# Last layer: the weighted sum of the gathered rows moved from GpSimd to VectorE, supertiles 1 to 7

## The chip, the cores and the metric

The kernel runs on one core of a Trainium2 chip, as one launch. The metric is the device time of that launch in microseconds (us). Three timed runs of the kernel before gave 674.5 us as the median, with 672.77 and 675.93 as the lowest and highest. The core has a matrix engine (TensorE, PE in the profile), VectorE (DVE), ScalarE (ACT), GpSimd (POOL) and SyncE (SP), which issues most DMAs. Each engine works through its own list of instructions in order; between engines, and between dependent instructions of one engine, the kernel waits on counting semaphores.

## The reference

A decoder block on 4096 tokens of width 128, float32: attention, a mixture of experts with two of eight experts for each token (routed by a second input, ctx), and a second mixture with eight of 32 experts and a shared expert. Each is applied to the normalised x and added to x.

```
x = x + attention(layernorm(x))
x = x + sum over the token's 2 experts of  weight * expert(layernorm(x))      # the sum that is moved
x = x + (sum over 32 experts of  c[t, e] * down_e(silu(gate_e(h)) * up_e(h)) + shared(h)),   h = layernorm(x)
```

The second line's last step is what the change touches: for each token t, `x[t] += w0[t] * y0[t] + w1[t] * y1[t]`, where y0 and y1 are the rows that its two experts computed. These lie in DRAM, sorted by expert (`y_sorted`), and are gathered by indirect DMA.

## The kernel before

**Tiling.** Tokens lie on the 128 partitions; 32 tiles of 128 tokens make up 8 supertiles of 512 (four tiles, TPS). `x_all` (128 x 32 x 128) holds x for the whole run. The last layer is a double loop over supertiles i = 0 to 7 and, within each, p = 0 to 16: 16 pairs of experts and the shared one (NC2 = 17). In a step n = 17 i + p TensorE makes a gate and an up product of three passes each (L1638 to L1640, over 128x512), ScalarE takes the silu of the gate (`r_s`, L975), VectorE multiplies it with the up product (`gated`, L1433: `rc_s`) and with the token weights (`weighted`, L1446: `t_s`; the shared expert has a plain copy instead, L1441). TensorE multiplies the result with the down weights; where it is split in a high and a low part (p from 5 to 16 in supertiles 1 to 6), ScalarE writes `t_h` (L740) and VectorE `t_l` (L1505) in front of that. TensorE may make the up product of step n only when `gated` of step n - 3 has freed its bank.

**Preparation of the next supertile.** While supertile i runs, the inputs of supertile j = i + 1 are prepared at steps fixed by the tables `SLOTS` and `FIRST` (L94, L98), each engine doing its part in its list at that step. For j of 2 and more:

- i = j - 2, early: GpSimd gathers the rows of j (`gather`, L682, 8 indirect DMAs, L688) into `yg[:, j % 2]`, then adds them to `x_all` (`combine(j, h)`, L700, for the two halves h of a supertile: 4 multiplications of 128x128, L705, and 2 additions of 128x256, L707, each with a wait for the one in front of it).
- i = j - 2, p = 14: VectorE waits for the sum and takes statistics of the four tiles (`row_statistics(j, 0)` and `(j, 1)`, L1346, BATCH_NORM_STATS2); at p = 15 `aggregate(j)` (L1352, BATCH_NORM_AGGREGATE) and GpSimd's `rstd(j)` (L693, an addition and a power).
- i = j - 1, p = 0: VectorE writes `nb`, the negated mean times the root (L1364). p = 1: ScalarE normalises four tiles (`xnp`, L918). p = 2: the expert weights of supertile j - 1 are turned and copied by ScalarE (`cT`, L740). p = 3: TensorE waits for `xnp` and for `cT` and turns `xnp` (L1540), ScalarE copies the result to `fxh` and VectorE makes its low part `fxl`. p = 6 to 12: the routing of j, with the routing's small instructions on VectorE at p = 9 to 12.

For j = 1 the same steps stand at p = 4 and later of supertile 0 (`FIRST`), and `combine(1, h)` is in front of them in GpSimd's list. Supertile 0 itself was combined in the layer before by VectorE (`combine_first`, L1448, 8 SCALAR_TENSOR_TENSOR at L1454, each computing weight times row plus x, with a wait behind each). GpSimd's list in the last layer holds `gather`, `combine` and `rstd` in the order gather(i + 2), combine(i + 2), rstd(i + 2). A `gather(j)` waits until the sum of j - 2 has freed its buffer.

Of the kernel before, what the change touches and what calls it, by code (L numbers as in the profile page):

```python
# [21 lines left out]
ALU = mybir.AluOpType  # L22
# [8 lines left out]
NS = T // ST  # L31
TPS = ST // P
# [69 lines left out]
def steps_at(i, p):  # L102

    steps = [(name, 1) for name, s in FIRST.items() if divmod(s, NC2) == (i, p)]
    return steps + [(name, j) for name, s in SLOTS.items() if name not in ("accS", "tp", "x2")
                    for j in [i + 1 - s // NC2] if s % NC2 == p and 2 <= j < NS]
# [52 lines left out]
def decoder_kernel(nc, x, ctx_in, W_DQ, b_DQ, W_UQ, b_UQ, W_DKV, b_DKV, W_UK, b_UK, W_UV, b_UV, W_QR, b_QR,  # L159
# [17 lines left out]
    with ExitStack() as stack:  # L177
# [11 lines left out]
        x_all = sb("x_all", [P, NT, D])  # L189
# [12 lines left out]
        wts = sb("wts", [P, NT, 2])  # L202
# [81 lines left out]
        yg = a("yg", [P, 2, TPS, 2, D])  # L284
# [44 lines left out]
        def sem(name):  # L329
            return stack.enter_context(nc.semaphore(name))  # L330
# [12 lines left out]
        s_yg = [[sem(f"gathered{i}_{h}") for h in range(2)] for i in range(2)]  # L343
# [19 lines left out]
        F = {n: sem("f2_" + n) for n in (  # L363
            "up gate act rc t th tl dn accS tp x2 cmb1 cmb bst pstat prstd pnb pxn pxT_ps fxh xT fxl lg lgS back sc cw c_ps cT "
            "chain").split()}
# [174 lines left out]
        def _(pool):  # L540
            ch = Chain(pool, s_pchain)
# [140 lines left out]
            def gather(j, t):  # L682
                if t == 0 and j <= 2:
                    stored(min(E1 * (j + 1), NBK))
                if j >= 2 and t == 0:
                    pool.wait_ge(F["cmb"], TPS + 2 * (j - 2))
                for c in range(2):
                    pool.indirect_dma_start(  # L688
                        out=yg[:, j % 2, t, c, :], out_offset=None, in_=ys,
                        in_offset=bass.IndirectOffsetOnAxis(ap=posi[:, j * TPS + t, c:c + 1], axis=0))\  # L690
                        .then_inc(s_yg0[t] if j == 0 else s_yg[j % 2][t // 2], 16)

            def rstd(j):  # L693

                pool.wait_ge(F["pstat"], j + 1)
                pool.tensor_tensor(mvp[:, :, 1], mvp[:, :, 1], meps[:, :], ALU.add).then_inc(F["prstd"], 1)  # L696
                pool.wait_ge(F["prstd"], 2 * j + 1)
                pool.tensor_tensor(mvp[:, :, 1], mvp[:, :, 1], mhalf[:, 0:TPS], ALU.pow).then_inc(F["prstd"], 1)

            def combine(j, h):  # L700
                pool.wait_ge(s_yg[j % 2][h], 64 * ((j + 1) // 2))
                t = slice(j * TPS + 2 * h, j * TPS + 2 * h + 2)
                for c in range(2):
                    for u in (2 * h, 2 * h + 1):
                        ch.done(pool.tensor_scalar(yg[:, j % 2, u, c, :], yg[:, j % 2, u, c, :],  # L705
                                                   wts[:, j * TPS + u, c:c + 1], 0.0, ALU.mult, ALU.add))
                    ins = pool.tensor_tensor(x_all[:, t, :], x_all[:, t, :], yg[:, j % 2, 2 * h:2 * h + 2, c, :], ALU.add)  # L707
                    if c == 0:
                        ch.done(ins)
                ins.then_inc(F["cmb"], 1)  # L710

            for b in range(2, NBK):
                w_high(b, 0)
                w1_low(b)
# [5 lines left out]
                    rstd(0)  # L720
            for t in range(TPS):
                gather(1, t)
            for h in range(2):
                combine(1, h)
            rstd(1)
            for i in range(NS):
                for p in range(NC2):
                    for name, j in steps_at(i, p):
                        if name == "prstd":
                            rstd(j)  # L730
                    if i + 2 < NS and p % 2 == 0 and p < 8:
                        gather(i + 2, p // 2)
                    if i + 2 < NS and p in (8, 9):
                        combine(i + 2, p - 8)


        @block.scalar
        def _(act):
# [49 lines left out]
            def normalise1(m, t):  # L788

                if m >= 2 and t == 0:  # L790
                    act.wait_ge(A["xT"], m - 1)
                at = m * TPS + t
                for part, (first, _) in enumerate(PARTS):
                    if at == first:
                        act.wait_ge(s_rstd1, part + 1)
                ins = act.activation(xn[:, m % 2, t, :], x_all[:, at, :], ACT.Identity, bias=nm1[:, at:at + 1],
                                     scale=mv1[:, at, 1:2])
                if t == TPS - 1:
                    ins.then_inc(A["xn"], 1)
# [214 lines left out]
        def _(dve):  # L1014
            tt, ts = dve.tensor_tensor, dve.tensor_scalar
            ch = Chain(dve, s_dchain)
# [269 lines left out]
            for n in range(-LEAD, NT + TAIL):  # L1286
# [3 lines left out]
                o, u, m = n - LAG["out"], n - LAG["sum"], n - LAG["xs"]  # L1290
# [53 lines left out]
            pc = Chain(dve, F["chain"])  # L1344

            def row_statistics(j, h):  # L1346
                dve.wait_ge(F["cmb"], TPS + 2 * (j - 1) + h + 1)
                for t in (2 * h, 2 * h + 1):
                    ins = dve.bn_stats(st6p[:, t, :], x_all[:, j * TPS + t, :])
                ins.then_inc(F["bst"], 1)  # L1350
# [62 lines left out]
            def route_weights(j):  # L1413
# [5 lines left out]
                if j >= 1:  # L1419
# [3 lines left out]
                    .then_inc(F["cw"], 1)  # L1423

            prep = dict(cmbA=lambda j: row_statistics(j, 0), cmbB=lambda j: row_statistics(j, 1), paggr=aggregate, pnb=negated_mean,
                        fxl=low_x, rt_a=route_groups, rt_b=route_rank, rt_c=route_experts, rt_d=route_weights)

# [58 lines left out]
            for n in range(NCB + LAG1 + 1):  # L1486
                b, c = n // FB, n % FB
# [507 lines left out]
```

## Time and profile before

| | before |
|---|---|
| median of three timed runs | 674.5 us |
| profiled execution, its own time | 673.04 us |
| its span (first to last instruction) | 671.0 us |
| TensorE busy | 618.0 us (92% of the span) |
| VectorE busy | 538.6 us (80%) |
| ScalarE busy | 422.2 us (63%) |
| GpSimd busy | 344.7 us (51%) |
| mean granted TensorE clock | 0.972 of full speed |

The last layer fills the span from about 354 us to its end. A page of the profile gives busy time by engine, the span in 40 slices, the DMA queues, the chain of work that ended last and the costliest groups of instructions. Instructions of one engine are pipelined: a new one can start before the record of the one in front ends, so the time that an instruction costs its engine is read from start to start. A row of the timeline gives the start in us, the duration in us, the engine and line, the operation, what it writes and reads, and in square brackets how long the engine was idle in front of it and what ended that.

### The profile page before, as it was taken

The numbers are of one execution on the slowest core, as the hardware profiler recorded it, in microseconds if no ns is written. First come the engines' busy times: TensorE is split into PE (matmuls) and PEld (weight loads), VectorE is DVE, ScalarE is ACT, GpSimd is POOL, SyncE is SP. The second block draws the span as 40 slices with busy tenths as digits, with TensorE's granted clock in tenths as the row PEclk, the third lists the DMA queues.
The fourth block names the chain that finished last, engine by engine and source line by source line (L and its number), as shares of the span: only waits on it lengthen the run. The fifth ranks groups of instructions, "written<-read, shape, count | busy, mean of one in ns | idle before, by whom it ended". The sixth has DMA issues, their size and how long they took to land.

```text
span 671.0 us, 11543 instructions
## 1 busy us (share of the span) xinstructions
PE 618.0 (92%) x3354; PEld 462.8 (69%) x3354; DVE 538.6 (80%) x1357; ACT 422.2 (63%) x779; POOL 344.7 (51%) x410
## 2 busy tenths in 40 slices
PE   8878888887879999999889999999999999999997
PEld 8655565554658888787667656776777767677873
DVE  4787799998866666876665778899999999989973
ACT  3674668764469998898875444665737465473530
POOL 6134868888775657864567672643808265000000
PEclk9988779999779999999999999999999999999999
DMA  8997013102445555554217543534536354434561
GB/s 224 311 384 246 17 60 96 33 32 64 107 111 156 163 174 167 179 165 149 81 60 195 127 99 113 152 101 133 138 108 164 96 155 117 133 106 127 146 157 32
DMA packets 77836, 90.20 MB, mean 134 GB/s; under 512 B 15361, under 2 KB 44011, under 8 KB 77774
## 3 DMA queue, kind: packets, MB, share of 16 engines
q1 hardware_dynamic: 72648, 80.96, 42.2%
q0 software_dynamic: 4288, 8.40, 4.4%
q8 instruction: 27, 0.44, 0.3%
q14 instruction: 35, 0.29, 0.1%
q10 hardware_dynamic: 838, 0.11, 0.1%
HBM read 64.48 MB, written 24.90 MB: 133 GB/s over the span
## 4 chain that ended last, share of the span: by engine, by line
PE 62%; POOL 11%; DVE 7%; issue 5%; ACT 2%; DMA 1%; DVEq 0%; ACTq 0%; POOLq 0%
PE bank L1638 10%; PE bank L1640 9%; PE bank L1639 9%; PE pair_banks L1929 7%; PE pair_banks L1540 5%; POOL x_sorted L613 5%; PE score_banks L1638 4%; PE score_banks L1640 4%; PE score_banks L1639 4%; PE pair_banks L1638 2%; PE pair_banks L1640 2%; PE pair_banks L1639 2%; POOL yg L688 2%; POOL sm L597 1%; DMA yg<-y_sorted,posi 1%
## 5 line engine op out<-in xcount | busy, mean ns | idle before, releaser
L975 ACT ACTIVATE r_s<-bank 128x512 f32<-128x512 f32 x136 | 80.7, 595 | 68.2 <-PE bank L1640 66.4
L1446 DVE TENSOR_TENSOR t_s<-rc_s,bcb 128x512 f32<-128x512 f32 x128 | 89.0, 698 | 4.8 <-PE pair_banks L1929 4.8
L613 POOL DMA_INDIRECT x_sorted<-xsb,posi x64 | 64.0, 1000 | 27.8 <-issue 14.8
L688 POOL DMA_INDIRECT yg<-y_sorted,posi x64 | 68.4, 1068 | 18.1 <-issue 17.7
L1433 DVE TENSOR_TENSOR rc_s<-r_s,score_banks 128x512 f32<-128x512 f32 x90 | 61.2, 680 | 17.9 <-ACT r_s L975 14.6
L1638 PE MATMUL bank<-fxh,Gh 128*128 128x512 f32 x136 | 73.2, 538 | 0.0
L740 ACT ACTIVATE t_h<-t_s 128x512 fp32r<-128x512 f32 x72 | 45.3, 629 | 41.3 <-DVE t_s L1446 26.6
L1929 PE MATMUL pair_banks<-t_s,Dn 128*128 128x512 f32 x128 | 63.2, 591 | 0.0
L1505 DVE TENSOR_TENSOR t_l<-t_s,t_h 128x512 fp32r<-128x512 f32 x72 | 54.9, 763 | 0.2
L1640 PE MATMUL bank<-fxh,Gl 128*128 128x512 f32 x136 | 53.7, 395 | 0.0
L1639 PE MATMUL bank<-fxl,Gh 128*128 128x512 f32 x136 | 53.4, 392 | 0.0
L1495 DVE TENSOR_TENSOR h1l<-bank,h1h 128x512 fp32r<-128x512 f32 x46 | 31.8, 691 | 21.9 <-ACT bank L962 21.9
L1495 DVE TENSOR_TENSOR h1l<-score_banks,h1h 128x512 fp32r<-128x512 f32 x46 | 31.8, 690 | 20.2 <-ACT score_banks L962 20.1
L696 POOL TENSOR_TENSOR mvp<-mvp,meps 128x4 f32<-128x4 f32 x8 | 1.6, 204 | 86.8 <-DVE mvp L1356 86.8
L597 POOL TENSOR_TENSOR sm<-sm,rden 128x512 f32<-128x512 f32 x29 | 30.2, 1043 | 19.1 <-DVE rden L1302 18.9
L740 ACT ACTIVATE uS<-pair_banks 128x256 f32<-128x256 f32 x32 | 12.3, 383 | 41.2 <-PE pair_banks L1725 36.1
L664 POOL TENSOR_SCALAR W2h<-wraw 128x512 fp32r<-128x512 f32 x21 | 13.0, 618 | 47.7 <-PE bank L1640 47.6
L1433 DVE TENSOR_TENSOR rc_s<-r_s,bank 128x512 f32<-128x512 f32 x46 | 31.3, 680 | 6.8 <-ACT r_s L975 5.6
L961 ACT ACTIVATE h1h<-score_banks,bcur 128x512 fp32r<-128x512 f32 x46 | 31.9, 694 | 7.0 <-PE score_banks L1640 3.3
L1638 PE MATMUL score_banks<-fxh,Uh 128*128 128x512 f32 x90 | 35.7, 396 | 0.6 <-DVE rc_s L1433 0.6
L1638 PEld LDWEIGHTS bank<-fxh,Gh 128*128 128x128 f32 x136 | 25.6, 188 | 15.4 <-issue 11.6
L1638 PE MATMUL bank<-h1h,W2h 128*128 128x512 f32 x92 | 36.1, 393 | 0.0
(335 smaller groups left out, 1847.3 us busy)
## 6 DMA issues: line engine op xcount, KB each, us to landing
bcb<-c_rows SPq DMA_DIRECT2D x128, 256.0 KB, 4.0
wraw<-in_L_xattn_W SPq DMA_DIRECT2D x46, 256.0 KB, 3.0
x_sorted<-wraw SPq DMA_DIRECT2D x1, 5888.0 KB, 18.3
y_sorted<-wraw SPq DMA_DIRECT2D x1, 5888.0 KB, 33.8
xg<-x_sorted SPq DMA_DIRECT2D x23, 256.0 KB, 2.6
y_sorted<-ysb SPq DMA_DIRECT2D x23, 256.0 KB, 2.0
ctxb<-in_ctx SPq DMA_DIRECT2D x8, 256.0 KB, 5.8
out<-x_all SPq DMA_DIRECT2D x8, 256.0 KB
```

The lines of the kernel that those rows point to most:

```text
L613: pool.indirect_dma_start(out=xs, out_offset=bass.IndirectOffsetOnAxis(ap=posi[:, m, c:c + 1], axis=0), in_=xsb[:, m % SC, :], in_offset=N ...
L688: pool.indirect_dma_start(out=yg[:, j % 2, t, c, :], out_offset=None, in_=ys, in_offset=bass.IndirectOffsetOnAxis(ap=posi[:, j * TPS + t, ...
L740: return act.activation(dst, src, ACT.Copy)
L975: act.activation(r_s[:, n % RB2, :], bank[n % 3][:, :], ACT.Silu).then_inc(F["act"], 1)
L1433: tt(rc_s[:, n % CB2, :], r_s[:, n % RB2, :], bank[3 + n % 3][:, :], ALU.mult).then_inc(F["rc"], 1)
L1446: tt(t_s[:, n % TB2, :], rc_s[:, n % CB2, :], bcb[:, p - 1, :], ALU.mult).then_inc(F["t"], 1)
L1495: tt(h1l[:, n % NB1, :], gate_bank1(n)[:, :], h1h[:, n % NB1, :].bitcast(F32), ALU.subtract)\
L1505: tt(t_l[:, k % HB2, :], t_s[:, m % TB2, :], t_h[:, k % HB2, :].bitcast(F32), ALU.subtract)\
L1638: mm(dst, wh, xh, start=start, stop=False)
L1639: mm(dst, wh, xl, start=False, stop=False)
L1640: return mm(dst, wl, xh, start=False, stop=stop)
L1929: ins = mm(bank[6][:, :], Dn[:, weights_of(p), :], t_s[:, n % TB2, :], start=(p == 0), stop=(p == NC2 - 1))
```

## The change

For supertiles 1 to 7 `combine` is taken out of GpSimd's list, definition and calls. `row_statistics(j, h)` on VectorE first waits for the gathered half, then issues four SCALAR_TENSOR_TENSOR of 128x128 (weight times row plus x, in place in `x_all`): two for the first expert, a wait, two for the second, and a wait in front of its two BATCH_NORM_STATS2. With two halves that makes eight such instructions and four waits for a supertile. They stand at p = 14 of supertile j - 2, and at p = 4 of supertile 0 for j = 1. `gather` and `rstd` stay on GpSimd, in the same order; all semaphores keep their counts.

```diff
--- before.py
+++ after.py
@@ -697,18 +697,6 @@
-            def combine(j, h):
-                pool.wait_ge(s_yg[j % 2][h], 64 * ((j + 1) // 2))
-                t = slice(j * TPS + 2 * h, j * TPS + 2 * h + 2)
-                for c in range(2):
-                    for u in (2 * h, 2 * h + 1):
-                        ch.done(pool.tensor_scalar(yg[:, j % 2, u, c, :], yg[:, j % 2, u, c, :],
-                                                   wts[:, j * TPS + u, c:c + 1], 0.0, ALU.mult, ALU.add))
-                    ins = pool.tensor_tensor(x_all[:, t, :], x_all[:, t, :], yg[:, j % 2, 2 * h:2 * h + 2, c, :], ALU.add)
-                    if c == 0:
-                        ch.done(ins)
-                ins.then_inc(F["cmb"], 1)
-
@@ -720,8 +708,6 @@
             for t in range(TPS):
                 gather(1, t)
-            for h in range(2):
-                combine(1, h)
             rstd(1)
@@ -730,8 +716,6 @@
                     if i + 2 < NS and p % 2 == 0 and p < 8:
                         gather(i + 2, p // 2)
-                    if i + 2 < NS and p in (8, 9):
-                        combine(i + 2, p - 8)
@@ -1344,6 +1328,15 @@
             def row_statistics(j, h):
+                dve.wait_ge(s_yg[j % 2][h], 64 * ((j + 1) // 2))
+                for c in range(2):
+                    for t in (2 * h, 2 * h + 1):
+                        xr = x_all[:, j * TPS + t, :]
+                        ins = dve.scalar_tensor_tensor(xr, yg[:, j % 2, t, c, :], wts[:, j * TPS + t, c:c + 1], xr,
+                                                       ALU.mult, ALU.add)
+                    if c == 0:
+                        pc.done(ins)
+                ins.then_inc(F["cmb"], 1)
                 dve.wait_ge(F["cmb"], TPS + 2 * (j - 1) + h + 1)
```

## Rows read from the trace of the kernel before

**Rows 1.** The page, busy us (share of span) xinstructions, TensorE and VectorE.

```profile
PE   618.0 (92%) x3354; PEld 462.8 (69%) x3354; DVE 538.6 (80%) x1357; ACT 422.2 (63%) x779; POOL 344.7 (51%) x410
```

**Rows 2.** Busy time by stretch: start:end, length, then us (xinstructions) of each engine.

```profile
core 0: us, PE busy (x) PEld busy (x) DVE busy (x) ACT busy (x) POOL busy (x), PEclk, DMA share, GB/s
493.00:532.00 39.00, 37.97 (x167) 28.76 (x166) 37.14 (x99) 22.74 (x41) 19.36 (x22) 1.00 0.49 130
...
571.00:610.00 39.00, 37.98 (x168) 28.66 (x167) 35.54 (x100) 22.66 (x42) 1.23 (x2) 1.00 0.45 119
```

**Rows 3.** Chain that ended last: start us, us, what; the turns at p = 3 and 14.

```profile
508.43 0.63 PE pair_banks L1540 x4
...
532.83 0.44 PE pair_banks L1540 x4
...
586.60 0.63 PE pair_banks L1540 x4
...
611.00 0.44 PE pair_banks L1540 x4
```

**Rows 4.** Timeline of all engines, supertile 3 p = 14 to supertile 4 p = 3.

```profile
498.84 0.87 DVE L1349 BATCH_NORM_STATS2 st6p<-x_all 128x6 f32<-128x128 f32 x4
...
505.28 0.17 DVE L1364 SCALAR_TENSOR_TENSOR nb<-mvp 128x4 f32<-128x4 f32 x1
...
505.48 1.65 ACT L918 ACTIVATE xnp<-x_all,nb,mvp 128x128 f32<-128x128 f32 x4 [1.37 <-DVE nb L1364]
...
508.03 0.26 ACT L740 ACTIVATE cT<-pair_banks 128x128 f32<-128x128 f32 x1
...
508.16 0.69 DVE L1433 TENSOR_TENSOR rc_s<-r_s,bank 128x512 f32<-128x512 f32 x1 [0.92 <-ACT r_s L975]
...
508.43 0.63 PE L1540 MATMUL pair_banks<-ident,xnp 128*128 128x128 f32 x4 [1.03 <-ACT cT L740]
```

**Rows 5.** Timeline of VectorE: the shared expert's copy in three supertiles, and an idle stretch.

```profile
406.94 0.77 DVE L1441 COPY t_s<-rc_s 128x512 f32<-128x512 f32 x1
...
446.25 0.42 DVE L1441 COPY t_s<-rc_s 128x512 f32<-128x512 f32 x1
...
523.43 0.69 DVE L1433 TENSOR_TENSOR rc_s<-r_s,score_banks 128x512 f32<-128x512 f32 x1 [0.38 <-ACT r_s L975]
524.04 0.83 DVE L1441 COPY t_s<-rc_s 128x512 f32<-128x512 f32 x1
```

**Rows 6.** Timeline of VectorE: SCALAR_TENSOR_TENSOR in the layer before, and in the routing.

```profile
267.82 0.96 DVE L1454 SCALAR_TENSOR_TENSOR x_all<-yg,wts,x_all 128x128 f32<-128x128 f32 x2
268.81 0.29 DVE L1457 BATCH_NORM_STATS2 st6p<-x_all 128x6 f32<-128x128 f32 x1
...
287.63 0.73 DVE L1454 SCALAR_TENSOR_TENSOR x_all<-yg,wts,x_all 128x128 f32<-128x128 f32 x2
288.39 0.29 DVE L1457 BATCH_NORM_STATS2 st6p<-x_all 128x6 f32<-128x128 f32 x1
...
497.44 0.29 DVE L1421 SCALAR_TENSOR_TENSOR cw<-rep,csum 128x128 f32<-128x128 f32 x1
497.64 0.68 DVE L1433 TENSOR_TENSOR rc_s<-r_s,score_banks 128x512 f32<-128x512 f32 x1
```

**Rows 7.** Timeline in supertile 0: VectorE's waits for the sums, GpSimd's for data.

```profile
360.67 0.48 DVE L1349 BATCH_NORM_STATS2 st6p<-x_all 128x6 f32<-128x128 f32 x2 [1.04 <-POOL x_all L707]
...
379.87 0.84 POOL L705 TENSOR_SCALAR yg<-yg,wts 128x128 f32<-128x128 f32 x2 [0.34 <-DMA yg<-y_sorted,posi]
...
383.63 0.49 DVE L1349 BATCH_NORM_STATS2 st6p<-x_all 128x6 f32<-128x128 f32 x2 [0.69 <-POOL x_all L707]
```

**Rows 8.** Timeline at the start of supertile 2: ScalarE's copy and the turn.

```profile
428.75 0.28 ACT L740 ACTIVATE cT<-pair_banks 128x128 f32<-128x128 f32 x1
...
430.64 0.60 PE L1540 MATMUL pair_banks<-ident,xnp 128*128 128x128 f32 x4
```

**Rows 9.** Timeline at the start of supertiles 1, 3, 5 and 6: the same turn.

```profile
392.10 0.63 PE L1540 MATMUL pair_banks<-ident,xnp 128*128 128x128 f32 x4 [0.98 <-ACT cT L740]
...
469.31 0.63 PE L1540 MATMUL pair_banks<-ident,xnp 128*128 128x128 f32 x4 [0.60 <-ACT cT L740]
...
547.51 0.63 PE L1540 MATMUL pair_banks<-ident,xnp 128*128 128x128 f32 x4 [1.01 <-ACT cT L740]
...
586.60 0.63 PE L1540 MATMUL pair_banks<-ident,xnp 128*128 128x128 f32 x4 [1.02 <-ACT cT L740]
```

## The prediction

> **What bounds the kernel now.** I read the page's busy times first, then the busy time by stretch, then the chain that ended last, then the timeline around each idle place of TensorE. TensorE is busy for 92% of the span [rows 1], and in the last layer for 37.97 us of 39 [rows 2]; VectorE shows 37.14 of 39 in the same stretch. So both are nearly full, and the question is where they are coupled. The chain gives the answer: it runs over TensorE except at one place in each supertile, the turn of `xnp` at p = 3. In rows 3 the turn at p = 3 is followed by the turn at p = 14 after 24.40 us (508.43 to 532.83, and 586.60 to 611.00), and that one by the next p = 3 after 14.69 us (532.83 to 547.51 in rows 9); together 39.09 us for a supertile.
>
> Rows 4 show what happens in the 14.69 us. VectorE takes the statistics at 498.84, writes `nb` at 505.28; ScalarE, idle for 1.37 us, starts `xnp` 0.20 us later; behind it in its list stand `t_h`, a silu and `cT`, which ends at 508.29; TensorE, idle for 1.03 us, turns `xnp` 0.14 us after that. Each step waits for the one in front. And VectorE is not idle between its catching up at 523.43 (the counterpart one supertile later, [rows 5]) and `nb`: the routing at p = 9 to 12 makes it late, and its next idle time is only the 0.92 us behind `nb` [rows 4]. So whatever is put into VectorE's list at p = 14 delays `nb`, the turn and with it TensorE, one for one. That idle time of TensorE is 0.98, 0.60, 1.03, 1.01 and 1.02 us at the start of supertiles 1, 3, 4, 5 and 6 [rows 4, 9], and none at the start of supertile 2, where `cT` ended at 429.03 and the turn came at 430.64 [rows 8]. With the 0.14 us of the others, that one has 1.47 us to spare.
>
> **The added work.** Eight SCALAR_TENSOR_TENSOR of 128x128 for each supertile. The same instruction with the same operands is in the trace, in the layer before: two of them, each with a wait behind it, take 0.76 us from start to start (287.63 to 288.39) while GpSimd idles, so 0.38 each [rows 6]. A wait costs some 0.12 of that: the routing's SCALAR_TENSOR_TENSOR of 128x128, 0.29 long, is followed after 0.20 by an instruction that needn't wait for it [rows 6]; taking that overlap of 0.09 and the 0.03 between end and next start off 0.38 leaves 0.26 without a wait (an estimate from these rows). Eight instructions, four with a wait: 4 x 0.38 + 4 x 0.26 = 2.56 us. The low end takes the routing's instruction, which has no pointer to a weight, 0.20 without and 0.29 + 0.03 with a wait: 2.1 us. The high end takes the pair that ran beside GpSimd's own work, 0.99 us for two (267.82 to 268.81), with every one waiting: 4.0 us. I take 2.56, since at p = 14 GpSimd only waits for VectorE. The statistics themselves stay, in two pairs in place of one four.
>
> **The removed work.** GpSimd loses 4 multiplications and 2 additions for each half. It has no wait behind it on the path, except in supertile 0: there VectorE waited 1.04 us (j = 1) and 0.69 us (j = 2) for the sum [rows 7]. Both waits go. Nothing else becomes late instead: GpSimd found the last half of j = 2 landed at 379.87, and VectorE wants it 2.6 us later and more. `gather(j)` for later j is issued behind `rstd(j - 1)`, so ahead of the `nb` at 505.28, for data wanted one supertile after the 498.84 of rows 4, over 30 us later. The waits that VectorE now makes on gathered data are therefore already met; behind one stand `gated` and all of TensorE, if I am wrong.
>
> **What GpSimd no longer disturbs.** While its multiplications and additions run, VectorE's instructions on two SBUF tensors, and its copy, take longer: the shared expert's copy takes 0.83 us at 524.04 and 0.77 at 406.94, against 0.42 at 446.25 [rows 5]. In sum VectorE is busy 37.14 us in a supertile with GpSimd's sums and 35.54 in one without, for as many instructions [rows 2]: 1.6 us. Only what lies behind VectorE's catching up counts for `nb`, and that is the copy: 0.41 us in supertiles 3 to 5, 0.35 in supertile 1, nothing in 2. The rest lies ahead of an idle stretch of VectorE, and the distance of 24.40 us from p = 3 to p = 14 is the same with the sums (508.43 to 532.83) and without (586.60 to 611.00) [rows 3].
>
> The Trainium skill (SBUF — State Buffer, section "SBUF: two separate sides") says that VectorE with two SBUF inputs and GpSimd lock each other out for a whole instruction. The trace agrees (the copy at 0.83 against 0.42). By that rule alone all 1.6 us of each supertile would come back; by rows 3 they do not reach TensorE. The rule's own result is the second rival.
>
> **The sum**, for the delay of TensorE:
> - j = 1, supertile 0, p = 4: 2.56 - 1.04 = 1.5 us. `nb` and the turn follow each other tightly there too.
> - j = 2, supertile 0, p = 14: 2.56 - 0.69 = 1.85 us (disturbances in supertile 0 not counted).
> - j = 3, supertile 1: 2.56 - 0.35 - 1.47 of spare time = 0.75 us.
> - j = 4, supertile 2: 2.56 us.
> - j = 5, 6, 7, supertiles 3 to 5: 3 x (2.56 - 0.41) = 6.45 us.
>
> Together 13.1 us. The delays don't overlap: each supertile's comes after VectorE has caught up, which it does between, since the 24.40 us from p = 3 to p = 14 hold idle time of VectorE and 1.2 us more of it than before. TensorE may show part of the new idle time earlier, as a wait for `gated` at p = 0 or 1 (its bank is freed three steps later), but not on top of it. Against the profiled execution's own 673.04 us that is 686.1; against the median of 674.5, 687.6. I take 686.5 us, 1.8% above the median.
>
> **The rivals.**
> - *The price is the low one* (2.1 us): 7 x 0.48 = 3.4 us less, 683 us. For it: 0.20 from start to start at this size [rows 6]. Against: the same instruction with its pointer had 0.38.
> - *The relief counts in full.* The 1.6 us of each of supertiles 1 to 5 come off, not 0.41: supertile 1 costs nothing, supertiles 2 to 5 0.96 each, with 3.35 of supertile 0: 7.2 us, 680.2 us. Needed for it: that VectorE's idle stretch at 523.43 is made by VectorE itself (ScalarE's `t_h` waits for `t_s`), so that all moves up. Against: the equal 24.40 us of rows 3.
> - *The price is the high one*, or a further wait comes on top, as for gathered data: 4.0 us each, 1.4 x 7 = 10 us more, 696 us.
> - *Faster*: GpSimd's late sums are what counted, and the additions on VectorE are hidden. Then 1.04 + 0.69 of waits [rows 7] and 0.35 + 3 x 0.41 of the copy go, 3.3 us, 669.7 us. It decides from the point at which VectorE has 2.56 us of idle time between the statistics and `nb`; the trace shows none there, and 0.92 us behind `nb`.
> - *No change*: idle time of VectorE behind `nb` and ahead of the routing takes most of the work, and what is left equals the 3.3 us: 674 us. It needs TensorE's idle time at the turn to have another cause than `nb`, as `cT`; but `cT` stands behind `xnp` in ScalarE's list, and ScalarE waited 1.37 us for `nb` [rows 4].
>
> **How the numbers follow.** Forecast (684 to 690 us) 0.62, low price 0.14, full relief 0.08, high price 0.07, no change 0.05, faster 0.04. The range from 680 to 691 us holds the first three, 0.84. About 0.5% is what a measurement of this kernel can tell from no change. Over 0.5% faster (below 671.1): 0.04. Within: 0.06, no change and a bit of the others. Slower: 0.90.
>
> **What would show it.** In the changed kernel: eight SCALAR_TENSOR_TENSOR at p = 14 that cost VectorE about 2.6 us; VectorE never idle from there to `nb`; ScalarE idle ahead of `xnp`; TensorE idle for about 3.2 us in front of or shortly ahead of the turn in supertiles 3 to 6, and 41.2 us from turn to turn there in place of 38.7 (430.64 to 469.31) and 39.1; the copy at 0.42 us everywhere; no wait of VectorE on a gather. The prediction is wrong if the turns stay 39.1 us apart (something hides the work), if the statistics come late because a gather does, or if the instructions take 0.2 or 0.5 us.

## The result and the profile after

The changed kernel takes 686.3 us (median of six timed runs, 684.56 to 687.62) against 673.69 us for the kernel before in the same measurement: a ratio of 1.0181, with a 95% interval of 1.0156 to 1.0206, so 12.6 us slower. The forecast was 686.5.

| | before | after |
|---|---|---|
| profiled execution's span | 671.0 us | 685.9 us |
| TensorE busy | 618.0 | 625.2 |
| VectorE busy | 538.6 | 546.3 |
| GpSimd busy | 344.7 | 288.0 |

The first lines of the page of the changed kernel (busy us, share of span, count; rows 1 before):

```profile
span 685.9 us, 11515 instructions
...
PE 625.2 (91%) x3354; PEld 465.7 (68%) x3354; DVE 546.3 (80%) x1413; ACT 422.2 (62%) x779; POOL 288.0 (42%) x326
```

VectorE has the 56 instructions more, and only 7.7 us more of busy time. The two spans differ by 14.9 us, 2.3 more than the medians. 1.45 us of that lie ahead of the layer that was changed (its first `gated` starts at 355.44 after 353.99), where the changed kernel has the same instructions. The granted TensorE clock differed there between the two executions (0.93 of full speed from 100 to 200 us before, and 0.88 after); that this makes the 1.45 us is likely, but not shown. From the first `gated` to the end it is 317.0 us before and 330.5 after: 13.4 us more.

The next rows are the turns of `xnp` at p = 3 in the changed kernel, on TensorE, at the start of supertiles 1 to 4 and 6 (rows 4, 8 and 9 before; the number in brackets is the idle time ahead):

```profile
396.56 0.63 PE L1533 MATMUL pair_banks<-ident,xnp 128*128 128x128 f32 x4 [0.96 <-ACT cT L724]
...
436.03 0.63 PE L1533 MATMUL pair_banks<-ident,xnp 128*128 128x128 f32 x4 [0.74 <-ACT cT L724]
...
477.31 0.63 PE L1533 MATMUL pair_banks<-ident,xnp 128*128 128x128 f32 x4 [1.62 <-ACT cT L724]
...
518.56 0.63 PE L1533 MATMUL pair_banks<-ident,xnp 128*128 128x128 f32 x4 [1.61 <-ACT cT L724]
...
601.48 0.63 PE L1533 MATMUL pair_banks<-ident,xnp 128*128 128x128 f32 x4 [1.60 <-ACT cT L724]
```

From 436.03 to 477.31 and from there to 518.56 it is 41.28 and 41.25 us, where the kernel before took 38.67 and 39.12. The timeline between, all engines, from p = 13 of supertile 3 to p = 3 of supertile 4 (the counterpart of rows 4):

```profile
505.78 0.68 DVE L1439 TENSOR_TENSOR t_s<-rc_s,bcb 128x512 f32<-128x512 f32 x1
...
506.38 1.26 DVE L1335 SCALAR_TENSOR_TENSOR x_all<-yg,wts,x_all 128x128 f32<-128x128 f32 x4
...
507.68 0.49 DVE L1342 BATCH_NORM_STATS2 st6p<-x_all 128x6 f32<-128x128 f32 x2
...
508.08 1.25 DVE L1335 SCALAR_TENSOR_TENSOR x_all<-yg,wts,x_all 128x128 f32<-128x128 f32 x4
...
509.36 0.49 DVE L1342 BATCH_NORM_STATS2 st6p<-x_all 128x6 f32<-128x128 f32 x2
...
510.49 0.50 PE L1631 MATMUL score_banks<-fxh,Uh 128*128 128x512 f32 x1 [0.94 <-DVE rc_s L1426]
...
515.42 0.16 DVE L1357 SCALAR_TENSOR_TENSOR nb<-mvp 128x4 f32<-128x4 f32 x1
...
515.61 1.65 ACT L902 ACTIVATE xnp<-x_all,nb,mvp 128x128 f32<-128x128 f32 x4 [1.36 <-DVE nb L1357]
...
518.16 0.26 ACT L724 ACTIVATE cT<-pair_banks 128x128 f32<-128x128 f32 x1
```

Four additions take 1.30 and 1.28 us from start to start, 2.58 for a supertile, and none waits for gathered rows. `nb` follows the first addition after 9.04 us; before, it followed the first statistics after 6.44 [rows 4]: 2.60 us more. ScalarE waits for `nb` as before (1.36 us), `cT` ends 0.14 us ahead of the turn as before. TensorE shows its new idle time in two places, 0.94 us for the `gated` that follows the additions and 0.58 more at the turn. These are 1.5 of the 2.1 us by which this supertile is longer (41.25 against 39.12); the other 0.6 us lie mostly in TensorE's own records, which show it busy for 38.6 us from turn to turn in place of 38.1 (the row at 510.49 shows 0.50 us, its counterpart before 0.39).

VectorE's counterpart of rows 5, one supertile on:

```profile
533.60 0.69 DVE L1426 TENSOR_TENSOR rc_s<-r_s,score_banks 128x512 f32<-128x512 f32 x1 [1.91 <-ACT r_s L959]
534.20 0.42 DVE L1434 COPY t_s<-rc_s 128x512 f32<-128x512 f32 x1
```

The copy is back at 0.42 us, and the idle time ahead of the `gated` in front of it has grown from 0.38 to 1.91 us: VectorE spends in idling what it no longer loses to GpSimd there, and then works without a pause into the turn.

### The profile page after: what moved, and what is told of

Read it like the earlier page. It is cut to its first block, busy times and chain, and to the rows that moved or that the text cites. A ratio compares the mean times of both kernels' runs of the same rounds, so it can differ in the third digit from the quotient of the medians.

```text
span 685.9 us, 11515 instructions
## 1 busy us (share of the span) xinstructions
PE 625.2 (91%) x3354; PEld 465.7 (68%) x3354; DVE 546.3 (80%) x1413; ACT 422.2 (62%) x779; POOL 288.0 (42%) x326
## 4 chain that ended last, share of the span: by engine, by line
PE 53%; DVE 19%; issue 7%; POOL 6%; ACT 3%; DMA 0%; DVEq 0%; ACTq 0%; POOLq 0%
PE bank L1631 8%; PE bank L1633 8%; PE bank L1632 8%; PE pair_banks L1922 5%; PE pair_banks L1533 5%; POOL x_sorted L613 4%; PE score_banks L1631 4%; PE score_banks L1633 3%; PE score_banks L1632 3%; DVE t_s L1439 2%; DVE x_all L1335 2%; DVE rc_s L1426 2%; PE pair_banks L1631 2%; PE pair_banks L1633 2%; PE pair_banks L1632 2%
## 5 line engine op out<-in xcount | busy, mean ns | idle before, releaser
L1439 DVE TENSOR_TENSOR t_s<-rc_s,bcb 128x512 f32<-128x512 f32 x128 | 87.3, 684 | 4.8 <-PE pair_banks L1922 4.8
L1498 DVE TENSOR_TENSOR t_l<-t_s,t_h 128x512 fp32r<-128x512 f32 x72 | 49.2, 684 | 0.2
L1633 PE MATMUL bank<-h1h,W2l 128*128 128x512 f32 x92 | 36.0, 392 | 0.0
```

Source lines behind the costliest of these rows:

```text
L1439: tt(t_s[:, n % TB2, :], rc_s[:, n % CB2, :], bcb[:, p - 1, :], ALU.mult).then_inc(F["t"], 1)
L1498: tt(t_l[:, k % HB2, :], t_s[:, m % TB2, :], t_h[:, k % HB2, :].bitcast(F32), ALU.subtract)\
L1633: return mm(dst, wl, xh, start=False, stop=stop)
```

## The experiments

Ten kernels, in three groups (half, double, nosum and ghost; pool12, the two nb_early kernels and sum_p8; the last two), each beside the kernel before on the same chip. The chips differ: the kernel before takes 673.75 us on that of the second group and 687.5 and 687.2 us on those of the first and the third. So each time is read against its own kernel before, as a ratio, and the expectations, which are given for a kernel before of 673.7 us, are turned into ratios. The changed kernel itself ran only on its first chip, so a comparison of another kernel with it goes over two ratios. A ratio comes from the single runs with its interval, and differs from the quotient of the two medians by up to 0.0016. The distance from turn to turn, from supertile 2 on, gives no sign of the difference between the chips; this table is worked out from the timelines of TensorE (us; "2 to 3": from the turn at the start of supertile 2 to that of 3).

| kernel | 2 to 3 | 3 to 4 | 4 to 5 | 5 to 6 | ratio to before (95%) |
|---|---|---|---|---|---|
| before | 38.67 | 39.12 | 39.08 | 39.09 | 1 |
| after | 41.28 | 41.25 | 41.46 | 41.46 | 1.0181 (1.0156 to 1.0206) |
| half | 39.97 | 39.98 | 39.97 | 39.98 | 1.0061 (1.0032 to 1.0090) |
| double | 43.90 | 43.89 | 43.90 | 44.41 | 1.0475 (1.0432 to 1.0519) |
| nosum | 38.98 | 38.99 | 39.00 | 39.01 | 1.0005 (0.9977 to 1.0033) |
| ghost | 42.06 | 41.77 | 42.51 | 42.25 | 1.0273 (1.0229 to 1.0316) |
| pool12 | 41.35 | 41.27 | 41.26 | 41.27 | 1.0152 (1.0107 to 1.0197) |
| nb_early_after | 39.78 | 39.80 | 39.95 | 40.00 | 1.0075 (1.0049 to 1.0101) |
| nb_early_before | 37.91 | 38.46 | 38.14 | 38.12 | 0.9940 (0.9915 to 0.9964) |
| sum_p8 | 39.17 | 39.31 | 39.29 | 39.31 | 1.0054 (1.0031 to 1.0078) |
| sum_p8_nb | 38.06 | 38.23 | 38.20 | 38.23 | 0.9977 (0.9946 to 1.0009) |
| pool12_p8_nb | 38.08 | 38.18 | 38.22 | 38.25 | 0.9937 (0.9906 to 0.9968) |

**Is it the additions?** Half of them, and twice as many. half leaves the second expert's rows out of the sum, double adds every row twice; neither computes the reference. The comments in the code shown from here on are added for the reader.

```
-                for c in range(2):
+                for c in range(1):                                   # half (its wait goes too)
+                for r, c in ((0, 0), (0, 1), (1, 0), (1, 1)):        # double (a wait behind each pair but the last)
```

> The changed kernel with the second expert's four additions of each supertile left out of the sum (so four instead of eight SCALAR_TENSOR_TENSOR, no wait between them). Theory (VectorE's list from its catching up to nb passes into TensorE's time one for one): 1.28 us less in each of six supertiles and the 0.93 us of supertile 1, 8.6 us less than the changed kernel's 686.3: about 677.7 us. Rival (VectorE loses its time waiting for gathered rows, not with the additions): no change, 686 us.

> The changed kernel with the whole sum made twice (16 additions for a supertile, a wait behind each group of two; x gets the rows twice). Theory: 2.56 us more in each of seven supertiles, 18 us more than 686.3: about 704 us. Rival (the 12.6 us of the change are a single cost for having moved the sum, such as the waits for gathered data): under 2 us more.

Measured: 1.0061 and 1.0475; expected were 677.7 / 673.7 = 1.0059 and 704 / 673.7 = 1.045. Half takes 1.3 us off the distance of the turns from supertile 2 to 4 (41.27 to 39.97), and double adds 2.6 (43.90). From 4 to 6, where the changed kernel has 41.46, it is 1.5 less and 2.4 to 3.0 more. On VectorE two additions with one wait take 0.64 us from start to start in half, and eight with four waits 2.60 in double: again 1.3 us for four. half still waits for the gathered rows, and yet the cost fell, and it rose with the number of additions. So neither a wait for these rows nor a one-time cost makes it.

**What did GpSimd's work cost?** Taken from both engines (nosum, which leaves the sum out and so doesn't compute the reference), and given back to GpSimd with nobody reading it (ghost).

```
# nosum, in row_statistics, in place of the four additions of a half
+                dve.memset(spare[:, :], 0.0).then_inc(F["cmb"], 1)
# ghost, on GpSimd for j = 2 to 7, where combine was
+                        ch.done(pool.tensor_scalar(gh_a[:, u % 2, :], yg[:, j % 2, u, c, :],
+                                                   wts[:, j * TPS + u, c:c + 1], 0.0, ALU.mult, ALU.add))
+                    ch.done(pool.tensor_tensor(gh_a[:, :, :], gh_a[:, :, :], yg[:, j % 2, 2 * h:2 * h + 2, c, :], ALU.add))
```

> The changed kernel with the sum left out on both engines for supertiles 1 to 7 (VectorE still waits for the gathered rows and signals with a one-element memset). Theory: the eight additions less at 0.1 us for the two memsets: 6 x 2.45 + 0.93 = 15.6 us less than 686.3, about 670.7 us, that is 3 us under the kernel before (its two waits for GpSimd and the disturbed copies). Rival (GpSimd's work on SBUF slowed the whole supertile by the 1.6 us by which VectorE's busy time falls): 1.7 + 5 x 1.6 = 9.7 us under the kernel before, 664 us.

> The changed kernel with GpSimd also making the multiplications and additions of supertiles 2 to 7 as before, but into a buffer that nobody reads. Theory: only the disturbed copy of the shared expert counts, 0.35 + 3 x 0.41 = 1.6 us more than 686.3: 687.9 us; the turns at p = 3 stand 0.4 us further apart in supertiles 3 to 5. Rival (relief counts in full): 5 x 1.6 = 8 us more, 694 us.

Measured for nosum: 1.0005 (0.9977 to 1.0033), where 0.9955 was expected and 0.986 by the rival. So both were too low, the rival by far more. The turns tell why: 38.98 us against 39.09. The two memsets cost more than the 0.1 us I gave them. In VectorE's timeline of nosum (p = 13 and 14 of a late supertile):

```profile
513.60 0.69 DVE L1432 TENSOR_TENSOR t_s<-rc_s,bcb 128x512 f32<-128x512 f32 x1
514.24 0.06 DVE L1332 MEMSET spare<- 128x1 f32 x1
514.34 0.49 DVE L1335 BATCH_NORM_STATS2 st6p<-x_all 128x6 f32<-128x128 f32 x2
514.78 0.06 DVE L1332 MEMSET spare<- 128x1 f32 x1
514.89 0.49 DVE L1335 BATCH_NORM_STATS2 st6p<-x_all 128x6 f32<-128x128 f32 x2
515.29 0.67 DVE L1419 TENSOR_TENSOR rc_s<-r_s,score_banks 128x512 f32<-128x512 f32 x1
```

From `t_s` to the next `gated` it is 1.69 us, where the kernel before needs 0.60 and 0.78:

```profile
498.24 0.68 DVE L1446 TENSOR_TENSOR t_s<-rc_s,bcb 128x512 f32<-128x512 f32 x1
498.84 0.87 DVE L1349 BATCH_NORM_STATS2 st6p<-x_all 128x6 f32<-128x128 f32 x4
499.62 0.67 DVE L1433 TENSOR_TENSOR rc_s<-r_s,score_banks 128x512 f32<-128x512 f32 x1
```

That leaves 0.31 us for two memsets with their waits. The turns give the same number: from supertile 2 to 3, where the copy of the kernel before was not disturbed, nosum has 38.98 us against 38.67. In the later ones 39.09 - 0.41 + 0.31 is 38.99, as measured. So in a supertile whose copy was disturbed, GpSimd's sum had cost TensorE 0.4 us, not 1.6. The memsets explain 0.2 us more in each supertile than I had allowed, 1.3 of the 3.4 us that the ratio misses; the other 2 us are as much as the interval leaves open, and no row places them. They may lie in supertile 0, whose expected gain can't be read here: from the turn within supertile 0 (that of j = 1) to the next it is 31 to 34 us on this chip in all kernels of the group, and 27 to 29 on that of the second.

Measured for ghost: 1.0273 (1.0229 to 1.0316), where 1.021 was expected and 1.030 by the rival. So the time of the whole kernel fits the rival's number and not that of my theory. The turns fit neither: from the turn of supertile 1 to that of 6 it took 208.7 us against 204.9 in the changed kernel, 3.8 more, where my theory had 1.6 and the rival 8. By the ratios ghost is some 6 us slower than the changed kernel, with an uncertainty of several us; what is beyond the 3.8 isn't placed.

Supertile by supertile the 3.8 us are 0.62, 0.78, 0.52, 1.05 and 0.79. The copy explains only the third, as foreseen (0.92 us at 504.61, next start 0.84 behind it); in the other four it took 0.41 or 0.42 us. VectorE's timeline of ghost in the fourth:

```profile
537.89 0.69 DVE L1437 TENSOR_TENSOR rc_s<-r_s,bank 128x512 f32<-128x512 f32 x1 [1.26 <-ACT r_s L970]
...
540.90 1.23 DVE L1509 TENSOR_TENSOR t_l<-t_s,t_h 128x512 fp32r<-128x512 f32 x1
...
543.30 1.23 DVE L1509 TENSOR_TENSOR t_l<-t_s,t_h 128x512 fp32r<-128x512 f32 x1
544.46 0.68 DVE L1437 TENSOR_TENSOR rc_s<-r_s,bank 128x512 f32<-128x512 f32 x1
545.05 0.73 DVE L1450 TENSOR_TENSOR t_s<-rc_s,bcb 128x512 f32<-128x512 f32 x1
545.70 1.24 DVE L1509 TENSOR_TENSOR t_l<-t_s,t_h 128x512 fp32r<-128x512 f32 x1
546.86 0.68 DVE L1437 TENSOR_TENSOR rc_s<-r_s,score_banks 128x512 f32<-128x512 f32 x1
547.46 0.41 DVE L1445 COPY t_s<-rc_s 128x512 f32<-128x512 f32 x1
```

and TensorE's:

```profile
565.19 0.50 PE L1642 MATMUL score_banks<-fxh,Uh 128*128 128x512 f32 x1 [2.06 <-DVE rc_s L1437]
...
573.27 0.63 PE L1544 MATMUL pair_banks<-ident,xnp 128*128 128x128 f32 x4 [1.61 <-ACT cT L735]
```

There is no idle time ahead of the `gated` at 546.86, where the changed kernel has 1.91 us. VectorE's last idle time is now the 1.26 us at 537.89, and three disturbed `t_l` (1.23 and 1.24 us) lie behind it, which my theory had in front of it. TensorE idles for 2.06 us behind them, where the changed kernel has 1.10. So the place of the last idle time was the wrong premise here: it moves when the engine gets more work. How much of the disturbance behind it arrives stays open: three times 0.55 us would be 1.65, and the distance grew by 1.05. The Trainium skill (SBUF — State Buffer, section "SBUF: two separate sides") has a VectorE instruction with two SBUF inputs and a GpSimd instruction that reads SBUF lock each other out. The trace agrees with it in the single instruction (1.24 against 0.68 us for `t_l`), and whether that reaches the end of the kernel depends on the idle time. The copy, on which the prediction rested its agreement, reads one tensor; that it is disturbed as well is what the rows show.

**The terms of supertile 0.** Sums of supertiles 1 and 2 back on GpSimd (pool12):

```
+            for h in range(2):
+                combine(1, h)
...
+                    if i == 0 and p in (8, 9):
+                        combine(i + 2, p - 8)
...
+                if j >= 3:                                           # VectorE's additions
```

> The changed kernel with the sums of supertiles 1 and 2 back on GpSimd, where they were before; 3 to 7 on VectorE. Theory: the two terms of supertile 0 go, 1.48 + 1.53 = 3.0 us: 683.3 us. Rival (the cost arises in the later supertiles only, since supertile 0 holds idle time): 686.3 us.

Measured: 683.12 us against 673.75 there, 1.0152 (1.0107 to 1.0197); 683.3 was expected, a ratio of 1.0143, and 1.0187 by the rival. Both lie in the interval, so the time doesn't decide. The turns do. The first two are at 10.91 and 38.06 us from the layer's start, as before (10.92 and 38.11), and 12.40 and 41.12 in the changed kernel. The two terms together are 3.0 us, and the rival falls.

**Is `nb` to the turn the path, or is VectorE simply full?** One number, `pnb`, moves `nb` from p = 0 to p = 16 of the supertile in front, in both kernels:

```
-SLOTS = dict(cmbA=-3, cmbB=-3, paggr=-2, prstd=-2, pnb=0, ...)
+SLOTS = dict(cmbA=-3, cmbB=-3, paggr=-2, prstd=-2, pnb=-1, ...)
```

> The changed kernel with one number changed: nb goes from p = 0 to p = 16 of the supertile before in VectorE's list (pnb = -1), in front of the gated, weighted and t_l of that step. Theory (nb, xnp, cT and the turn are the path): nb 1.8 us earlier, xnp 1.36 us earlier, since ScalarE's silu ahead of it then ends last; that takes 1.36 us off the turn's idle time of 1.6 in supertiles 3 to 6, and the 0.74 and 0.96 of two others: 7.1 us less, about 679 us. Rival (VectorE's whole work in a supertile is the bound, wherever it stands): 686.3 us.

> The kernel before with the same one number changed (pnb = -1). Theory: TensorE's idle time at the turns goes, 0.98 + 0.60 + 1.03 + 1.01 + 1.02 = 4.6 us: 669.1 us against 673.7. Rival (another thing than nb holds the turn, as cT or the down products): no change.

Measured: 678.6 us and 669.73 us, against 679 and 669.1 expected and no change by the rivals. The timeline of nb_early_after, all engines:

```profile
507.02 1.03 POOL L698 TENSOR_TENSOR mvp<-mvp,mhalf 128x4 f32<-128x4 f32 x1
...
508.35 0.17 DVE L1357 SCALAR_TENSOR_TENSOR nb<-mvp 128x4 f32<-128x4 f32 x1
...
508.88 1.64 ACT L902 ACTIVATE xnp<-x_all,nb,mvp 128x128 f32<-128x128 f32 x4
...
511.42 0.26 ACT L724 ACTIVATE cT<-pair_banks 128x128 f32<-128x128 f32 x1
...
511.83 0.63 PE L1533 MATMUL pair_banks<-ident,xnp 128*128 128x128 f32 x4
```

`nb` stands right behind GpSimd's power, ScalarE no longer idles ahead of `xnp`, and TensorE no longer ahead of the turn. The distance of the turns is 39.8 to 40.0 us in place of 41.25 to 41.46. Of what is left over the 38.1 of the kernel before with `nb` early, 0.9 to 1.3 us are TensorE's waits for `gated` (and once `t_l`) behind the additions; the rest lies mostly in TensorE's own records.

**The same work elsewhere in VectorE's list.** Sum and statistics of supertiles 3 to 7 at p = 8, where VectorE had its idle time (sum_p8):

```
-                    for j in [i + 1 - s // NC2] if s % NC2 == p and 2 <= j < NS]
+                    for j in range(2, NS) for at in [s - 6 if name in ("cmbA", "cmbB") and j >= 3 else s]
+                    if i + 1 - at // NC2 == j and at % NC2 == p]
```

> The changed kernel with the sum and the statistics of supertiles 3 to 7 six steps earlier, at p = 8 in place of 14, in front of the gated for which VectorE idles 1.9 us there (at 533.60 in the changed kernel's trace). Theory (only VectorE's work behind its last idle time counts): the idle time takes 1.9 us of the sum in supertiles 2 to 5, supertile 1 loses its 0.93: 8.5 us less, 677.8 us. Rival (VectorE's whole work is the bound): no change, 686.3 us. A third outcome, slower than 686.3: the gathered rows haven't landed by p = 8 and VectorE waits for them.

Measured: 677.25 us, 677.8 expected, 686.3 by the rival. In its timeline of VectorE the additions have taken the idle time's place:

```profile
523.33 0.67 DVE L1499 TENSOR_TENSOR t_l<-t_s,t_h 128x512 fp32r<-128x512 f32 x1
523.93 1.25 DVE L1336 SCALAR_TENSOR_TENSOR x_all<-yg,wts,x_all 128x128 f32<-128x128 f32 x4
525.21 0.49 DVE L1343 BATCH_NORM_STATS2 st6p<-x_all 128x6 f32<-128x128 f32 x2
525.62 1.25 DVE L1336 SCALAR_TENSOR_TENSOR x_all<-yg,wts,x_all 128x128 f32<-128x128 f32 x4
526.90 0.49 DVE L1343 BATCH_NORM_STATS2 st6p<-x_all 128x6 f32<-128x128 f32 x2
527.30 0.67 DVE L1427 TENSOR_TENSOR rc_s<-r_s,score_banks 128x512 f32<-128x512 f32 x1
527.89 0.42 DVE L1435 COPY t_s<-rc_s 128x512 f32<-128x512 f32 x1
```

No wait for gathered rows stands ahead of them, and the turns are 39.3 us apart: the same instructions on the same engine cost 2 us less for each supertile. That is the idle time they fill: 2.58 - 1.91 leaves 0.67 us, and 39.3 us is 0.6 more than the 38.7 that the kernel before would have with its copy undisturbed.

**Both moves together**, without and with the sums of supertiles 1 and 2 on GpSimd.

> The changed kernel with both moves: sum and statistics of supertiles 3 to 7 at p = 8, nb at p = 16. Theory: from the turn of supertile 2 on TensorE waits for nothing at the turns, as in the kernel before with nb early (38.1 to 38.5 us from turn to turn); what is left of the change is supertile 0, 1.5 + 1.5 us: 669.7 + 3 = 672.7 us. Rival (with eight additions more, VectorE's whole work bounds the supertile once the places of the steps do not): 39 us and more from turn to turn, 677 us and more.

> As the other, with the sums of supertiles 1 and 2 back on GpSimd. Theory: the time of the kernel before with nb early, 669.7 us, whether the sums of 3 to 7 stand on GpSimd or on VectorE; so under both kernels. Rival: slower than 673.7 us, since VectorE carries 2.6 us more in each of five supertiles.

Measured: 0.9977 (0.9946 to 1.0009), with 672.7 / 673.7 = 0.9985 expected, and 0.9937 (0.9906 to 0.9968), with 0.994 expected. The turns are 38.1 to 38.25 us apart, with no idle time of TensorE between them from supertile 2 on. The rivals (39 us and more, and slower than the kernel before) fall. Busy time by stretch in pool12_p8_nb, two stretches of 39 us:

```profile
core 0: us, PE busy (x) PEld busy (x) DVE busy (x) ACT busy (x) POOL busy (x), PEclk, DMA share, GB/s
479.00:518.00 39.00, 39.00 (x173) 29.26 (x171) 38.29 (x108) 23.53 (x44) 13.91 (x12) 1.00 0.52 132
518.00:557.00 39.00, 39.00 (x172) 29.30 (x170) 38.29 (x108) 23.51 (x44) 14.20 (x11) 1.00 0.51 132
```

VectorE carries the eight additions of each of these supertiles and is busy for 38.29 of 39 us, more than in the changed kernel (37.74 of 41.25 from turn to turn), and still TensorE is the bound. So with the steps well placed the move of the sums of supertiles 3 to 7 shows neither gain nor cost: 0.9937 with them on VectorE, 0.9940 with all on GpSimd, each some 4 us under its own kernel before. These two were measured on different chips, with intervals of some 2 us either way. The sums of supertiles 1 and 2 still cost something on VectorE: 0.9977 against 0.9937, on the same chip.

## Why the prediction was right, point by point

- **The bound and the coupling.** Right: TensorE, held at the turn by `nb`, `xnp` and `cT`, with VectorE never idle from p = 8 to `nb`. The two kernels with `nb` early show the path by removing it, sum_p8 shows that the place in VectorE's list counts and not its total. TensorE shows 2.55 to 2.9 us of idle time in supertiles 2 to 5, not the 3.2 foretold; the rest is in its longer records.
- **The price.** 2.56 us predicted, 2.58 measured. The nearest row was the same instruction with the same operands in the layer before, and taking only the undisturbed pair was right: at p = 14 GpSimd waited for VectorE. The split into 0.38 with a wait and 0.26 without is not seen by itself; only its sums are (0.64 for two in half, 2.58 for eight).
- **The waits on gathered rows** were met, as expected, at j = 1 and 2 as well.
- **j = 1:** 1.5 us predicted, the first turn is 1.48 later. **j = 2:** 1.85 predicted, 1.53 measured; the prediction had left out the disturbance in supertile 0, and it was there: the routing's small instruction that writes `grep` took 0.44 us at 379.13 before, and 0.19 at 382.06 after, 0.25 of the 0.32 us.
- **j = 3** (supertile 1, with spare time): 0.75 predicted, 0.93 measured.
- **j = 4:** 2.56 predicted, 2.61 measured. **j = 5:** 2.15 predicted, 2.13 measured. **j = 6 and 7:** 2.15 each predicted, 2.38 and 2.37 measured. In these TensorE also waits 0.16 us for a `t_l` ahead of the turn, which the kernel before didn't show.
- **The sum:** 13.1 us predicted for the layer, 13.4 measured in the profiled execution, 12.6 between the medians. That the forecast of 686.5 lies 0.2 us beside the 686.3 is partly luck. It was set between two starting points, and the kernel before came out at 673.69 where the prediction had 674.5; and the terms missed by -0.3 to +0.2 us each, partly against each other.
- **Where I was too sure:** that GpSimd's disturbance of VectorE counts only through the copy. It does in the two kernels compared, as the turns of nosum show. In ghost it came to 3.8 us from turn to turn in place of 1.6, since VectorE's last idle time lay further ahead, and to some 6 in the whole time, of which the rest isn't placed.

## What to carry to other kernels

To price an instruction added to an engine, look for that engine's last idle time ahead of the next hand-over on the path: put in front of it the work is free up to the length of the idle time, behind it it costs its full length, however busy the engine is over all. Before moving work off an engine or onto it, look whether one number in the order of the steps does more: here an early `nb` gave 4 us, and the placement of the same additions and their statistics decided about 9. The relief that an engine gets from a quiet neighbour is only worth what lies behind its last idle time. When more work uses that idle time up, more of it counts (3.8 us in ghost, where the whole would have been 8).

## What the runs showed of the hardware

VectorE was busy for 38.29 of 39 us without becoming the bound, which I had not expected of lists in order with buffers of three banks between two engines. The chips of the first and third group needed 13.4 to 13.8 us more for the kernel before. Some 10 us of that lie ahead of the last layer: its first `gated` starts at 363.0 to 364.4 us in the traces from these chips, and at 352.8 to 355.4 in the others. A part lies in supertile 0: in half, ScalarE stood idle for 6.65 us there ahead of one small copy, with nothing of the kernel's own named as the cause:

```profile
385.49 0.28 ACT L724 ACTIVATE lgS<-pair_banks 128x128 f32<-128x128 f32 x1 [6.65 <-remote]
```

The same copy shows 3.71 us in nosum, 6.70 in sum_p8_nb and 4.19 in pool12_p8_nb, and 0.94 to 0.96 on the chips of the changed kernel and of the second group. What it waited for stays open; from supertile 2 on the distances of the turns on these chips fit those of the other.
